# Second layer of a graph network: conditioned rows made from the plain rows in two VectorE passes

## The reference, cut to what matters

```python
def _cond_layer_norm(x, cond, sw, sb, bw, bb):
    mu = jnp.mean(x, axis=-1, keepdims=True)
    var = jnp.var(x, axis=-1, keepdims=True)
    xn = (x - mu) * jax.lax.rsqrt(var + EPS)
    scale = cond @ sw + sb
    bias = cond @ bw + bb
    return xn * (1.0 + scale) + bias
...
for i in range(NUM_BLOCKS):
    y = _cond_layer_norm(x, cond, s1_w[i], s1_b[i], b1_w[i], b1_b[i])
    y = _sparse_attention(y, src, dst, wq[i], bq[i], wk[i], bk[i], wv[i], bv[i], wo[i], bo[i])
    x = x + y
    y = _cond_layer_norm(x, cond, s2_w[i], s2_b[i], b2_w[i], b2_b[i])
    y = jax.nn.relu(y @ m_w1[i] + m_b1[i]) @ m_w2[i] + m_b2[i]
    x = x + y
```

## Time and profile before

| | value |
|---|---|
| median of the runs | 2424.24 us (2418.73 to 2425.98) |
| profiled execution, its span | 2423.89 us, 2422.1 us |
| mean granted TensorE clock | 0.945 of full speed |
| TensorE (PE) busy | 2113.5 us, 87% of the span |
| VectorE (DVE) busy | 1607.4 us, 66% |
| ScalarE (ACT) busy | 1021.8 us, 42% |
| GpSimd (POOL) busy | 644.7 us, 27% |

### The profile page before, as it was taken

How to read it: one execution, slowest core, us unless ns; L and a number is a source line. 1 busy time by engine, 2 the same in 40 slices (tenths; PEclk the granted TensorE clock), 3 DMA queues, 4 the chain that set the end, 5 groups by cost and what they waited for, 6 DMA issues and landing times. The chain is left out here.

```text
span 2422.1 us, 38711 instructions
## 1 busy us (share of the span) xinstructions
PE 2113.5 (87%) x14446; PEld 1597.9 (66%) x14446; DVE 1607.4 (66%) x3166; ACT 1021.8 (42%) x1498; POOL 644.7 (27%) x472
## 2 busy tenths in 40 slices
PE   6888979998899998799899799999798996888784
PEld 5885537887777887677788677788685554333331
DVE  8995354878564877564778554778555045899964
ACT  1112224666343666343666343666330031244442
POOL 0000025100554100543200543200520000376763
PEclk9999989999899999999999999999899997998886
DMA  1011311889420889421788511778845000000001
GB/s 58 34 45 46 103 36 48 152 142 166 91 67 26 145 143 157 105 60 33 131 146 158 116 42 51 122 144 153 193 95 142 17 14 8 1 0 0 1 0 42
DMA packets 488314, 195.74 MB, mean 81 GB/s; under 512 B 441241, under 2 KB 457625, under 8 KB 488133
## 3 DMA queue, kind: packets, MB, share of 16 engines
q1 hardware_dynamic: 488133, 193.31, 38.8%
HBM read 62.94 MB, written 25.45 MB: 36 GB/s over the span
## 5 line engine op out<-in xcount | busy, mean ns | idle before, releaser
L670 PE MATMUL psum<-turned_probability_parts,values_high 125*128 125x125 bf16 x1600 | 287.3, 224 | 55.8 <-DMA turned_probability_parts<-probability_parts 27.0
L862 DVE CUSTOM_DVE_ANT_0 probabilities<-psum,counts 125x1250 f32<-125x1250 f32 x160 | 233.6, 1460 | 128.7 <-PE psum L672 128.3
L1393 ACT ACTIVATE probabilities<-probabilities,row_peaks 125x1250 f32<-125x1250 f32 x160 | 214.6, 1342 | 178.2 <-DVE row_peaks L866 178.2
L672 PE MATMUL psum<-turned_probability_parts,values_low 125*128 125x125 bf16 x1600 | 286.7, 224 | 0.0
L671 PE MATMUL psum<-turned_probability_parts,values_high 125*128 125x125 bf16 x1600 | 286.6, 224 | 0.0
L1587 DVE SCALAR_TENSOR_TENSOR probability_parts<-probabilities,row_masses,probability_parts 125x1250 bf16<-125x1250 f32 x160 | 246.0, 1538 | 8.9 <-ACT probability_parts L1403 8.3
L1914 POOL TENSOR_TENSOR logs_and_shifts<-logs_by_source,target_shifts_spread 125x1250 f32<-125x1250 f32 x80 | 208.1, 2617 | 128.7 <-ACT target_shifts_spread L2047 69.4
L1403 ACT ACTIVATE probability_parts<-probabilities,row_masses 125x1250 bf16<-125x1250 f32 x160 | 214.2, 1338 | 40.0 <-DVE row_masses L874 34.4
L2153 PE MATMUL psum<-probabilities_turned,values_and_ones 125*65 125x512 f32 (+1 forms) x480 | 199.0, 561 | 21.8 <-ACT probabilities_turned L2064 11.4
L670 PEld LDWEIGHTS psum<-turned_probability_parts,values_high 125*128 125x128 bf16 x1600 | 161.1, 101 | 77.4 <-issue 75.5
L453 ACT ACTIVATE norm_std<-norm_moments,norm_eps 125x1 f32<-125x1 f32 x120 | 35.3, 295 | 331.9 <-DVE norm_moments L449 331.9
(11 more groups left out here) (292 smaller groups left out, 5155.8 us busy)
## 6 DMA issues: line engine op xcount, KB each, us to landing
weight_stage<-in_L_gnn_m_w SPq DMA_DIRECT2D x32, 256.0 KB, 2.6
block_inputs_kept<-nodes SPq DMA_DIRECT2D x8, 896.0 KB
counts_kept<-counts_by_target_rows SPq DMA_DIRECT2D x10, 625.0 KB, 3.6
logs_kept<-counts SPq DMA_DIRECT2D x1, 5468.8 KB
nodes<-block_inputs_kept SPq DMA_DIRECT2D x12, 448.0 KB
turned_probability_parts<-probability_parts SPq DMA_TRANSPOSE x320, 3.6
counts_by_target<-counts_kept SPq DMA_DIRECT2D x2, 2187.5 KB
logs_by_source<-logs_kept SPq DMA_DIRECT2D x1, 4375.0 KB
```

Of the source, the lines that this page charges most:

```text
L670: pe.matmul(out, lh, rh, start=first, stop=False, skip_group_check=True)
L672: return pe.matmul(out, ll, rh, start=False, stop=last, skip_group_check=True)
L862: dve.tensor_tensor_reduce(prob[0:TILE, T % 2, :], scores, fx.count_src[0:TILE, i, 0:NODES], scale, MASKED, ALU.add, ALU.max, p[:, 0:1]).t ...
L1393: nc.scalar.activation(prob[0:TILE, T % 2, :], prob[0:TILE, T % 2, :], ACT.Exp, bias=fx.peak[0:TILE, T % 2, 1:2], accum_out=fx.mass[0:TILE ...
```

## The change: what it does

The normed tile and its ScalarE instruction go away, and so does the small VectorE instruction for the shift. `finish` reads the plain tile instead. Its first pass is (row - mean) times (1 + scale), its second is that times the inverse deviation plus the bias. Both passes now take a column (mean, inverse deviation) beside their tile in SBUF and their bank of PSUM.

The 1 of 1 + scale comes from TensorE: row 17 of `condition_weights` (COND + 1, for the scale matrix alone) is set to 1.0. For this GpSimd clears the tile with one instruction and then runs an `affine_select` over 32x512 elements of it, and the first load waits for both.

```diff
-        xn = place("normed_rows", [128, 2, DIM], F32)
...
-            for k in range(2):
-                pool.memset(raw[:, k, :], 0.0).then_inc(w_ready, 1)
+            pool.memset(raw[:, :, :], 0.0).then_inc(w_ready, 1)
+            pool.wait_ge(w_ready, 1)
+            pool.affine_select(out=raw[:, 0, :], in_=raw[:, 0, :], compare_op=ALU.not_equal, fill=1.0,
+                               base=-(COND + 1), pattern=[[0, DIM]], channel_multiplier=1).then_inc(w_ready, 1)
...
-            def normed(b, ph, t):
-
-                act.wait_ge(shift_ready, 20 * b + 10 * ph + t + 1)
-                nc.scalar.activation(xn[0:TILE, t % 2, :], fx.nodes[0:TILE, t, :], ACT.Identity,
-                                     bias=fx.shift[0:TILE, t % 2:t % 2 + 1],
-                                     scale=fx.rstd[0:TILE, t % 2:t % 2 + 1]).then_inc(xn_ready, 1)
...
-                    if norm_at(bp, s - 1):
-                        normed(*norm_at(bp, s - 1))
...
-                dve.wait_ge(rstd_own, L + 1)
-                dve.scalar_tensor_tensor(fx.shift[0:TILE, k], fx.moments[0:TILE, t % 2, 0:1], -1.0, fx.rstd[0:TILE, k],
-                                         ALU.mult, ALU.mult).then_inc(shift_ready, 1)
...
-                dve.wait_ge(xn_ready, L + 1)
                 if L >= 2:
                     dve.wait_ge(y_turned, L - 1)
                 dve.wait_ge(mod_ready, L + 1)
-                dve.scalar_tensor_tensor(yr[0:TILE, t % 2, :], bank(0)[0:TILE], 1.0, xn[0:TILE, t % 2, :],
-                                         ALU.add, ALU.mult).then_inc(finish_own, 1)
+                dve.wait_ge(var_ready, L + 1)
+                dve.scalar_tensor_tensor(yr[0:TILE, t % 2, :], fx.nodes[0:TILE, t, :], fx.moments[0:TILE, t % 2, 0:1],
+                                         bank(0)[0:TILE], ALU.subtract, ALU.mult).then_inc(finish_own, 1)
                 dve.wait_ge(finish_own, L + 1)
-                dve.tensor_tensor(yr[0:TILE, t % 2, :], yr[0:TILE, t % 2, :], bank(1)[0:TILE],
-                                  ALU.add).then_inc(y_ready, 1)
+                dve.wait_ge(rstd_own, L + 1)
+                dve.scalar_tensor_tensor(yr[0:TILE, t % 2, :], yr[0:TILE, t % 2, :], fx.rstd[0:TILE, t % 2:t % 2 + 1],
+                                         bank(1)[0:TILE], ALU.mult, ALU.add).then_inc(y_ready, 1)
```

More of the change, by code:

```diff
@@ L743, in second_layer @@
         rstd_own = sem("rstd_own")
-        shift_ready = sem("norm_shift_ready")
-        xn_ready = sem("normed_rows_ready")
         y_ready = sem("y_ready")
```

## The result

The changed kernel takes 2398.26 us (median of 4 runs, 2396.74 to 2400.95). The kernel before, timed beside it, takes 2421.48 (2414.15 to 2425.98). The ratio is 0.9908 with a 95% interval of 0.9893 to 0.9922: faster by 19 to 26 us. The forecast was 2406 with a range of 2400 to 2416.

A forecast was written before the change was run, and what follows sets the result against it. TensorE, busy 87% of the span, was taken as the bound, with 33.1 us of waits for conditioned tiles; 13.2 + 2.8 + 0.4 + 3.4 - 0.3 - 0.8 = 18.7 us off 2423.9 gave 2405.2, forecast as 2406, range 2400 to 2416.

The forecast's parts named there:

- first steps after attention, idle: TensorE's 14.8 us of waits in four blocks' early second-norm steps shrink to 0.1 for each of 16 tiles: 13.2 us gained.
- the clock there: After attention in blocks three and four, shorter waits leave TensorE's clock up: 2 x 1.4 = 2.8 us gained, bounds 0 and 2.8.
- tile 8: Wait of 1.6 us once per block; only the shift's 0.17 less the passes' 0.12 counts: 0.4 us gained, bounds 0 and 1.
- next first norm: First norm of the following block, three times: waits partly removed, 3 x 1.15 = 3.4 us gained, bounds 1.5 and 5.
- ahead of the first block: The 4.8 us wait stays and three tiles pay for dearer passes: 0.3 us lost, bounds 0.4 lost and 1 gained.
- start: Second layer's beginning, TensorE idle 11.46 us: the larger select on GpSimd costs 0.8 us with the wait, bounds 0.5 and 1.4.
- all the rest of the span: Everything outside the summed stages: no gain or loss was counted when 18.7 us were taken from the profiled 2423.9.
- The main step: In early steps after attention VectorE's list sets the pace; the change cuts its 4.99 us to 3.94, against TensorE's 3.90.
- No wait of TensorE for `slot_a` or `nodes`: Such new waits would show the gain lost to late perceptron weights or bias rows: 2422 us, chance 0.10.
- TensorE's own share of a step: Distance of two transposes less the wait, in a step after attention: 644.90 - 639.91 - 1.09 = 3.90 us.
- VectorE's step: Reciprocal to reciprocal after attention: 4.99 - 0.89 (shift) - 0.28 (ScalarE wait) + 0.12 (dearer passes) = 3.94 us.
- the slow step behind the 2.1 us wait: In the third block a 5.29 us step without a wait, against 3.90, read as matmuls at the lower clock.

## Why the prediction was right, and why the time fell outside

Term by term, forecast against the profile of the changed kernel:

| term | forecast | measured |
|---|---|---|
| first steps after attention, idle | 13.2 | 13.1 |
| the clock there | 2.8 | 1.9, with what each wait costs beyond its idle |
| tile 8 | 0.4 | -0.1 |
| next first norm | 3.4 | 4.9 |
| ahead of the first block | -0.3 | +0.3 |
| start | -0.8 | -0.7 |
| sum | 18.7 | 19.5 |
| all the rest of the span | 0 | 3.4 |

**The main step was right**: VectorE's list made these tiles late, and without the shift and the normed tile TensorE's own step is what is left; the passes last 0.74 and 0.75 us and are not held. The split of that step was not right. It gave the shift 0.89 us of a step and the wait for ScalarE 0.28, but kept alone the normed tile costs as much as the shift (18 and 17 us). The wait at the block's start and at tile 8 is unchanged, as said. No wait of TensorE for `slot_a` or `nodes` took the place of the removed one.

**What was mis-sized.** TensorE's own share of a step was taken as 3.90 us, the distance of two transposes less the idle time. It is 3.74. A wait costs more than its idle: with an idle of 0.36 the step is 4.26, with 1.09 it is 4.99, so 0.16 on top in both; with 0.21 it is 4.07, 0.12 on top. The transposes behind a wait last 0.65 us and without one 0.59. VectorE's step was taken as 3.94 and is 3.72: it is then paced by TensorE, and `turned_low` starts 0.05 us after the reciprocal and not 0.16. This is why of each of the next first norm's two early waits more went than forecast: its first three steps are 4.59, 3.73 and 6.53 us, where they were 4.68, 4.76 and 6.53, and tile 8 there 4.06 against 4.54. That term, forecast at 3.4 and measured at 4.9, is the one of the sum that was most too small.

**The clock was right in sign, not in its reason.** The prediction took the slow step behind the 2.1 us wait as something that goes with the wait. The matmuls at the low level (0.43 us apart and not 0.23) are still there, at another place. TensorE's rows at the first block's output product in the changed kernel:

```profile
622.42 0.76 PE L670 MATMUL psum<-slot_b_high,turned_high 128*125 128x512 f32 x1 [0.79 <-issue]
622.98 0.63 PE L671 MATMUL psum<-slot_b_low,turned_high 128*125 128x512 f32 x1
623.41 0.63 PE L672 MATMUL psum<-slot_b_high,turned_low 128*125 128x512 f32 x1
...
626.34 0.39 PE L670 MATMUL psum<-slot_b_high,turned_high 128*125 128x512 f32 x1
```

The kernel before had such a stretch once in each block: at the output product in blocks 1 and 2, behind the 2.1 and 2.0 us waits in blocks 3 and 4, 32 matmuls in sum that are 0.43 us or more apart. The changed kernel has it at the output product in all four, 28 matmuls. So 4 x 0.2 = 0.8 us of the 1.9 went with slow matmuls; the other 1.1 has to come from what the waits cost beyond their idle, and wasn't split further. Even the 0.8 is luck of this pair of profiles: at the lower level these stretches spent 15.3 and 15.1 us in the two profiles of before, and 13.6, 6.6 and 18.2 in the three of the changed kernel. In the second profile of the kernel before only the fourth block has the long wait and the slow matmuls behind it:

```profile
1736.71 0.65 PE L1142 MATMUL psum<-identity,conditioned_rows 125*128 125x125 f32 x4 [2.60 <-DVE conditioned_rows L1469]
1742.00 0.59 PE L1142 MATMUL psum<-identity,conditioned_rows 125*128 125x125 f32 x4
```

Where the stretch falls changes from run to run of the same kernel; why, no run shows. In the first profile of before it made little difference: from the first output product to tile 9 a block took 61.5, 61.1, 61.6 and 60.9 us, with a fast product and a 2.1 us wait or with a slow product and a 1.1 us one. In the second a block with no slow stretch took 60.5 us, and one with both 63.7. Now a fast product counts for more: 55.9 and 55.8 us in two blocks of the second profile, 57.3 to 57.8 in the other two and in the first profile.

**Tile 8** gave nothing, for a reason that was not seen: the 0.33 us of the shift there is taken by the hidden layer's low part for the most part. Counted from the transposes of tile 7 (670.87 and 670.80 us) it starts 0.38 us earlier, still beside a GpSimd instruction, lasts 0.28 us longer, and so ends only 0.10 us earlier. VectorE's rows, before and after:

```profile
672.89 0.33 DVE L1456 SCALAR_TENSOR_TENSOR norm_shift<-norm_moments,norm_rstd 125x1 f32<-125x1 f32 x1
...
673.74 1.19 DVE L1516 TENSOR_TENSOR turned_low<-hidden_rows,turned_high 128x1000 fp32r<-128x1000 f32 x1
```
```profile
673.29 1.47 DVE L1504 TENSOR_TENSOR turned_low<-hidden_rows,turned_high 128x1000 fp32r<-128x1000 f32 x1
```

It has two tensors in SBUF, as the shift had. The passes' 0.12 us take the rest. The prediction had counted the shift's median of 0.17 us there and no change of the low part.

**Why outside the range.** The step that failed is the last one, from the sum to a time: 18.7 us were taken from a profiled 2423.9, and all the rest of the span was put at nothing, with no room for it in the range. Step by step the forecast of 2405.2 (written as 2406) becomes the measured time so. The stages gave 0.8 us more than the sum, with terms off both ways and the next first norm, where TensorE's step of 3.74 us had been taken as 3.90, the most: 2404.4. The rest of the span was 3.4 us shorter in this pair of profiles, though its instructions are the same (its largest part went with the clock in the last layers, as shown above): 2401.0, and the profiled execution took 2400.95, inside the range. The median of the four runs lies another 2.7 us below the profiled one, 2398.26. The kernel before moved likewise: with a fourth run its median fell from 2424.24 to 2421.48. The lower end of the range, 2400, lay 1.4 us under all upper ends of the terms (2423.9 - 22.5 = 2401.4), and the rest alone went from 1961.2 to 1970.9 over all profiles. So the miss is mostly scatter that the range left out, and 0.8 us of it is the terms. Whether attention, 2.0 us shorter in this pair, holds a small effect of the change stays open.

## What to carry to other kernels

When an engine is late by a chain of small instructions, count the chain, not the work: a column of 125 numbers cost 0.96 us in one step, more than the 0.69 of a pass over 125x512, because it was held. On VectorE write such a column with one tensor and a column operand (212 to 218 ns here, never held), since with two tensors in SBUF it waited until GpSimd's running instruction had ended (up to 2.08 us). A removed wait is worth its idle and a little more (0.12 to 0.16 us here), and the next thing to try is what else stands ahead of the late instruction and isn't urgent: two moved low parts per block took 378.6 - 372.9 = 5.7 us off the norms' stages. Give the range room for the stages that the change does not touch; two more profiles of the same kernel show how much.

## What had not been expected of the hardware

A column operand in SBUF goes with 0.05 to 0.06 us more in a pass over 512 elements (0.69 to 0.74 and 0.75) and 0.05 in one of a single element (0.161 to 0.214), and none of these instructions was held. The second pass and the single element also changed the kind of instruction; only in the first pass it stayed the same. One select over 32x512 takes 0.60 us, twice one over 128x128 and less than the four times of its length; one clearing of 32x1024 takes 0.94:

```profile
343.61 0.94 POOL L1026 MEMSET condition_weights<- 32x1024 f32 x1 [136.72 <-POOLq L480]
...
344.70 0.60 POOL L1028 TENSOR_SCALAR_AFFINE_SELECT condition_weights<-condition_weights 32x512 f32<-32x512 f32 x1
...
352.38 1.21 PE L1131 MATMUL psum<-condition_weight_parts,condition_parts 96*125 96x512 f32 x2 [12.16 <-POOL condition_weight_parts L1020]
```

It is the counterpart of the earlier trace rows: from the clearing to the first modulation 8.77 us, where it was 8.06.
